# A macaron block's attention stage on one core: the two half substitutions one behind the other, a gram and four tap loads moved

## The reference

```
x = x + 0.5 * ffn(layernorm(x))
x = x + attention(layernorm(x))
x = x + 0.5 * ffn(layernorm(x))
```

```
q, k, v = silu(dwconv4(x @ Wq)), silu(dwconv4(x @ Wk)), silu(dwconv4(x @ Wv))
beta = sigmoid(x @ Wb);  q, k = l2norm(q), l2norm(k);  v, kb = v * beta, k * beta
attn = where(strict_lower, -(kb @ k.T), 0)          # one 32x32 matrix per chunk and head
T = inv(eye(32) - attn);  u = T @ v;  w = T @ kb     # unit triangular inverse
# then over the 8 chunks of a sequence, in order:
u_i = u - w @ S;  o_i = q @ S + where(lower, q @ k.T, 0) @ u_i;  S = S + k.T @ u_i
# o, v and three depthwise filters of v (3, 15, 64 taps) are five paths; their statistics
# and x go through a small gate network; the paths are mixed, normalised, projected by Wo
```

## Time and profile before

| | us |
|---|---|
| three runs, median (lowest to highest) | 455.55 (454.15 to 456.23) |
| profiled execution, its own time | 455.75 |
| its span, first to last instruction | 454.0 |

### The profile page before, as it was taken

One profiled execution on the slowest core, in us unless ns is written; L12 is line 12 of the kernel. 1 busy time (PEld: TensorE's weight loads), 2 busy tenths in 40 slices (PEclk: granted clock), 3 DMA queues, 4 the chain that ended last, 5 costly groups with the idle time before them and its releaser, 6 DMA issues.

```text
span 454.0 us, 9783 instructions
## 1 busy us (share of the span) xinstructions
PE 382.7 (84%) x4132; PEld 285.7 (63%) x4132; DVE 302.1 (67%) x461; ACT 277.5 (61%) x434; POOL 42.8 (9%) x103
## 2 busy tenths in 40 slices
PE   5599999999999799596699667936789696969996
PEld 3377776678866677495578656522256575647885
DVE  2796779547145678579849769287867696658533
ACT  4788948888597467155244306337278749457973
POOL 4000000000000100048870000000000000000000
PEclk9899999999999979679675675877689888979999
DMA  8900009200000000700060000070000000001001
GB/s 275 311 1 2 2 1 254 72 1 2 0 1 0 3 2 7 204 4 1 17 196 6 3 4 4 1 253 2 0 1 1 1 1 2 0 1 48 3 1 46
DMA packets 14325, 19.75 MB, mean 44 GB/s; under 512 B 960, under 2 KB 9152, under 8 KB 14272
## 3 DMA queue, kind: packets, MB, share of 16 engines
q1 hardware_dynamic: 14128, 18.94, 13.9%
q10 hardware_dynamic: 144, 0.01, 0.0%
HBM read 17.91 MB, written 1.05 MB: 42 GB/s over the span
## 4 chain that ended last, share of the span: by engine, by line
PE 57%; DVE 25%; ACT 10%; issue 6%; DMA 1%; DVEq 0%; SPq 0%; ACTq 0%
PE ps_a L726 11%; PE ps_a L727 11%; PE ps_a L824 6%; PE ps_a L870 3%; PE ps_d L856 2%; PE ps_a L882 2%; DVE arena L1069 2%; PE ps_a L915 2%; DVE arena L1072 2%; PE ps_d L892 2%; PE ps_d L791 2%; PE ps_a L913 2%; PE ps_a L928 2%; PE ps_d L727 2%; PE ps_d L726 2%
## 5 line engine op out<-in xcount | busy, mean ns | idle before, releaser
L726 PE MATMUL ps_a<-acts,w_f 128*128 128x512 f32 x256 | 104.2, 407 | 8.3 <-ACT acts L600 7.7
L727 PE MATMUL ps_a<-acts,w_f 128*128 128x512 f32 x256 | 102.1, 399 | 0.0
L726 PEld LDWEIGHTS ps_a<-acts,w_f 128*128 128x128 f32 x256 | 49.5, 194 | 22.0 <-ACT acts L600 9.7
L727 PEld LDWEIGHTS ps_a<-acts,w_f 128*128 128x128 f32 x256 | 49.5, 193 | 11.0 <-issue 0.7
L600 ACT ACTIVATE acts<-ps_a,vec 128x512 fp32r<-128x512 f32 x64 | 44.5, 696 | 0.0
L824 PE MATMUL ps_a<-xnp,conv_w 128*128 128x512 f32 x156 | 38.4, 404 | 0.0
L1138 DVE TENSOR_TENSOR acts<-gbuf,acts 128x512 fp32r<-128x512 f32 x32 | 21.6, 690 | 24.9 <-ACT acts L600 24.9
L1138 DVE TENSOR_TENSOR acts<-ghbuf,acts 128x512 fp32r<-128x512 f32 x32 | 21.2, 689 | 20.8 <-ACT acts L600 20.8
L824 PEld LDWEIGHTS ps_a<-xnp,conv_w 128*128 128x128 f32 x156 | 29.5, 189 | 8.5 <-issue 1.7
L985 DVE SCALAR_TENSOR_TENSOR arena<-ps_d,arena 128x512 f32<-128x512 f32 x16 | 11.0, 687 | 28.5 <-ACT arena L554 26.3
L597 ACT ACTIVATE gbuf<-ps_a,vec 128x512 f32<-128x512 f32 x32 | 22.3, 696 | 11.1 <-PE ps_a L727 11.1
(11 more groups left out here) (211 smaller groups left out, 798.5 us busy)
## 6 DMA issues: line engine op xcount, KB each, us to landing
toep<-in_fir SPq DMA_DIRECT2D x24, 288.0 KB, 5.6
w_in<-in_h SPq DMA_DIRECT2D x4, 1024.0 KB, 8.1
g_rows<-in_gW SPq DMA_DIRECT2D x4, 640.0 KB, 6.8
w_in<-in_w SPq DMA_DIRECT2D x6, 256.0 KB, 4.1
iobuf<-in_x SPq DMA_DIRECT2D x4, 256.0 KB, 6.6
toep<-in_taps SPq DMA_DIRECT2D x1, 768.0 KB, 6.5
y<-iobuf SPq DMA_DIRECT2D x3, 256.0 KB, 2.4
toep<-in_proj SPq DMA_DIRECT2D x1, 256.0 KB, 9.2
```

Source lines behind the costliest of these rows:

```text
L726: e.matmul(bank, w, hi, start=start, stop=False)
L727: return e.matmul(bank, w, lo, start=False, stop=stop)
```

## The change

Three moves, and one new wait on each of two queues. Half 0's gram (and its turn) go behind `qkv 3`, the last convolution tile; `sumsq 2` keeps its place on ScalarE and VectorE but is issued by TensorE between the first and the second quarter of `qkv 3`. VectorE does 4 steps of half 0's substitution in `solve 0` instead of 11 and 23 in `solve 2` instead of 16. GpSimd starts half 1's substitution only once `xt 0` is done (`inv_done` 1). SyncE loads tap groups 2 and 3 only once gram 1 is done. All twelve `token` steps and the eight `window` steps now stand before `fir` 4 to 7 of the order; `turn4` and the first squares stand between the `yy` steps; `xt 1` goes from before `first 0` to behind `rec 1`, and the `yy` and `aq` steps of half 1 each go one place back, so that `aq 6` follows `turn3 0`.

```diff
-SPLIT = 11
+SPLIT = 4
...
-    s += [("qkv", 2, 2), ("gram", 2, 0), ("lmat", 2, 0), ("window", 2, 4), ("window", 2, 5), ("sumsq", 2, 2),
-          ("qkv", 2, 3), ("solve", 2, 0), ("window", 2, 6), ("window", 2, 7), ("sumsq", 2, 3)]
+    s += [("qkv", 2, 2), ("window", 2, 4), ("window", 2, 5), ("sumsq", 2, 2), ("qkv", 2, 3), ("gram", 2, 0), ("lmat", 2, 0),
+          ("window", 2, 6), ("window", 2, 7), ("solve", 2, 0), ("sumsq", 2, 3)]
...
-    s += [("token", 2, i) for i in (0, 1, 4, 5, 8, 9)] + fir[4:6]
-    s += [("token", 2, i) for i in (2, 3, 6, 7, 10, 11)] + fir[6:8]
-    s += [("window", 2, i) for i in range(8, 16)]
-    for k in range(4):
-        s += [("yy", 2, k), fir[8 + k]]
-    s += [("turn4", 2, 0), ("sq", 2, 0), ("turn4", 2, 1), ("sq", 2, 1)] + sums(0) + [("sq", 2, 2)] + sums(1)
+    s += [("token", 2, i) for i in (0, 1, 4, 5, 8, 9, 2, 3, 6, 7, 10, 11)]
+    s += [("window", 2, i) for i in range(8, 16)] + fir[4:8]
+    s += [("yy", 2, 0), fir[8], ("yy", 2, 1), fir[9], ("turn4", 2, 0), ("turn4", 2, 1), ("sq", 2, 0)]
+    s += [("yy", 2, 2), fir[10], ("sq", 2, 1), ("yy", 2, 3), fir[11]] + sums(0) + [("sq", 2, 2)] + sums(1)
...
-    s += [("bo", 2, b) for b in range(4)] + [("sq", 2, 5)] + sums(4) + [("sq", 2, 6), ("xt", 2, 1)]
-    ahead = [("yy", 2, k) for k in range(4, 8)] + [("aq", 2, k) for k in range(4, 8)]
+    s += [("bo", 2, b) for b in range(4)] + [("sq", 2, 5)] + sums(4) + [("sq", 2, 6)]
+    ahead = [("xt", 2, 1)] + [("yy", 2, k) for k in range(4, 8)] + [("aq", 2, k) for k in range(4, 8)]
...
-    s += [("turn3", 2, 0), ("sq", 2, 7), ("aq", 2, 7), ("bo", 2, 4), ("bo", 2, 5), ("bo", 2, 6)]
+    s += [("turn3", 2, 0), ("sq", 2, 7), ("aq", 2, 6), ("aq", 2, 7), ("bo", 2, 4), ("bo", 2, 5), ("bo", 2, 6)]
...
             load_toep(e, 1)
+            e.wait_ge(S["pe_d"], D_AT[("gram", 2, 1)] + H)
...
             e.wait_ge(S["l_turned"], 1)
+            e.wait_ge(S["inv_done"], 1)
...
+                        if i == 3 and w == 0:
+                            sumsq(2)
-                elif kind == "sumsq":
+                elif kind == "sumsq" and i != 2:
+                    sumsq(i)
```

More of the change, by code:

```diff
@@ L767, in wo, with sumsq @@
                 e.matmul(take_d(D_AT[("wo", 2, i)]), wo_w[:, :], tile(o_c, i % 2), start=True, stop=True).then_inc(S["pe_d"], 1)
+            def sumsq(i):
+                for w in range(2):
+                    e.wait_ge(S["act_ss"], 2 * i + w + 1)
+                    e.matmul(take_d(D_AT[("sumsq", 2, i)] + w), head_w[:, :], qs[:, 6 + 2 * w + i % 2], start=True, stop=True
+                             ).then_inc(S["pe_d"], 1)
             e.wait_ge(S["consts"], 1)
```

## The result

Over the timed runs the changed kernel takes 448.34 us (median of 4, 447.03 to 449.53), the kernel before 455.25 us (median of 4); the ratio is 0.9848, 95% interval 0.9827 to 0.9869.

The account below looks back on a forecast made before the run. A chain of waits through TensorE and VectorE bounds the kernel. Early gains go nearly all back to GpSimd at `xt 1`; shorter work behind it brings `turn 0` 3.4 us earlier: profiled 455.75 becomes 452.35, forecast 452.2, range 450.2 to 456.2.

Parts of the forecast that it names:

- The waits that the prediction named: TensorE's 0.68 us before gram 0, its 4.36 in gram 1, and some 3 forecast for `xt 1` on GpSimd.
- three signs of being wrong: Gram 1's wait over 3 us, GpSimd over 38 us, or `turn3 0` more than 18 us behind `xt 1`'s end.
- Gram 0 behind `qkv 3`: Stretch ahead of gram 1: gram 1 starts at 182.7, gain 1.6 us, bounds 0 and 2.3.
- Taps behind gram 1: In gram 1: instruction wait falls to about 1.1 us, 6.9 against 10.1, gain 3.2, bounds 0 and 4.36.
- all but 0.14: Chance 0.14 went to the rival that gram 1's wait belongs to its position and stays: 3.2 us lost, 455.4.
- VectorE alone: `solve 2` up to `xt 0`: steps 8 to 30 without GpSimd take 17.8 us; `xt 0` ends at 212.9, 6.2 earlier.
- GpSimd: Half 1's substitution, started at 213.0: takes 36.8 us (bounds 36.8 and 39.3), ends at 249.9, 13.7 later than before.
- The rival that VectorE's transposes and reductions slow it: From 213 to 250: VectorE's other work slows GpSimd, ending 6.9 us later, time 459.1; chance 0.10.
- Behind `xt 1`: From `xt 1`'s end: 16.9 us to `turn3 0`, `turn 0` at 276.1 instead of 279.51; bounds 0 and 6.
- The low clock at `yy 4`: Rival: TensorE idles before `yy 4`, the clock stays low behind `xt 1`, costing 3.0 us, time 455.2; chance 0.10.

Follow-up runs that it names:

- the second profile: The changed kernel run again unchanged, against the kernel before: 449.34 us, ratio 0.9882 (0.9853 to 0.9910).

## Why the prediction was wrong

The direction was right and the size half. Two terms of the sum were too small, the gram's move (1.6 us, measured 3.4) and the taps (3.2, measured 4.5 and 3.8). The waits that the prediction named are the ones that the traces show, and none of its three signs of being wrong came, since none of them looked at the stretch ahead of gram 1.

For the first step, windows with the columns of the earlier trace rows: windows 4 and 5 and then `sumsq 2`, first in the kernel before, then in the changed one.

```profile
160.00:161.80 1.80, 1.80 (x13) 1.70 (x10) 1.22 (x2) 0.98 (x2) 0.00 (x0) 0.50 0.00 0
161.80:164.40 2.60, 2.60 (x6) 1.05 (x5) 2.07 (x3) 2.36 (x3) 0.00 (x0) 0.50 0.02 6
...
151.80:152.50 0.70, 0.70 (x8) 0.70 (x7) 0.67 (x2) 0.59 (x3) 0.00 (x0) 1.00 0.00 0
155.50:156.70 1.20, 1.20 (x4) 0.52 (x3) 0.00 (x0) 0.57 (x2) 0.00 (x0) 1.00 0.00 0
```

Step by step:

- **Gram 0 behind `qkv 3`** (1.6 us, bounds 0 and 2.3): the step that failed. It gave 3.4 us (31.21 to 27.84 and 27.81), outside its own bounds, in both profiles, and undoing it gave exactly that stretch back (31.24). I let TensorE's stretch shrink by the 0.68 us wait alone, since the low clock "now falls on `sumsq 3`". But windows 4 and 5 and `sumsq 2` now run at the full clock, ahead of `qkv 3` and inside it, and take 2.1 us together instead of 4.4. Windows 6 and 7 and `sumsq 3` got the low clock in their place, but lost only 0.9 us (from 173.99 to 177.27 before, from 168.88 to 173.10 now). Gram 0 is 0.9 us shorter (163.55 to 168.94, 5.4 us against 6.3), and the 0.68 us wait is gone. In all `sumsq 3` ended 21.2 us behind `qkv 2` (173.17 - 151.93), not 23.5. VectorE was then the one that ended last, with no idle time before 174.92: from gram 0's end to its first row of tile 3 it took 6.0 us, and my sum had 6.2. That sum was right, but it hung on a gram 0 that I let end 18.3 us behind `qkv 2`; it ended 17.0 behind it.
- **Taps behind gram 1** (3.2 us, gram 1 in 6.9): 4.5 and 3.8 (5.64 and 6.35). The term was mis-sized by adding two things that exclude each other, the 4.25 us of running at the low clock and a wait of 1.1. At the full clock it is 2.99 + 1.16 + 1.49, at the low one 4.54 + 0.16 + 1.50: one or the other hides. That it is the loads that hold TensorE back, which I gave all but 0.14, is shown from both sides (0.9901 with the wait alone, 0.9989 without it). The border of the instruction block was put near its place: 1.7 us into gram 1 by the prediction, and the packet starts 1.8 us into it (2.6 in the second profile).
- **VectorE alone** (23.3 to `xt 0`): 23.5. Right; steps 8 to 30 took 18.25 us (188.77 to 207.02) where I had 17.8.
- **GpSimd** (36.8 us, bounds 36.8 and 39.3): 246.46 - 209.10 = 37.4. Right within 0.6 us; `xt 1` waited 3.60 us, forecast about 3. The rival that VectorE's transposes and reductions slow it does not hold. Most of the 0.6 is a false mirror: I took steps 0 to 14 to cost as much as steps 16 to 30, but with none of VectorE's substitution beside them they take 18.15 us (209.10 to 227.25) and the others 17.68. So of the 18.81 us that steps 0 to 14 took beside VectorE only 0.7 were lost to it, not 1.2. The rule that the prediction cites from the Trainium skill ("SBUF — State Buffer", Who interferes with whom) agrees: between 209 and 246 us VectorE has no instruction with two inputs in SBUF and GpSimd is not slowed, while each multiply and subtract of its substitution has two. (The section leaves VectorE's two-port modes out of what it says on one input, which the prediction does not say.)
- **Behind `xt 1`** (16.9, then 7.25): 16.4 and 16.7, then 7.4 and 7.7. Near. The low clock at `yy 4` came (0.50 from 248.50 to 250.30), but did not lengthen the stretch. No run took the three instruction blocks away by themselves, so that they make up this gain is argued, not shown.

The rest of the distance to 448.34 I take for luck of one set (the second gave 5.1 us of gain, where the six stretches say 4.9 to 6.0). My range was too narrow below for a sum whose two largest terms were both taken at the low side.

What stays open: the taps wait alone is worth 4.5 us and the whole change 5.1 to 6.9, so the gram's move, the split, GpSimd's wait and the order bring 0.6 to 2.4 together, and the intervals do not tell more. Without the gram move they seem to cost something: 0.9952 against 0.9901 for the taps alone, in one set, with intervals that just overlap. The profiles say the same and show where it goes. The kernel before with the tap wait alone has 121.4 us in the six stretches, the changed kernel 120.4 and 121.5. Up to `xt 0`'s end the changed kernel is 4.0 to 4.7 us ahead of it, and from there to `turn 0` it falls back by 3.7 to 4.1, since it waits for GpSimd.

## What to carry to other kernels

When TensorE stands in a run of small matmuls and the trace calls it "issue", look at the DMA share beside it and at the packets of the instruction queue before anything else: moving a bulk load behind that run was worth more here than all the reordering of work. Parts of a schedule can be worth nothing or less one by one and pay only together (the gram's move needed the small split, the small split needed GpSimd late, GpSimd late needed `xt 1` behind `rec 1`), so price each under the others; the last of these links rests on the rows of two kernels, not on a run with that order alone undone. And re-read who ends last after each step: the wait moved from GpSimd to ScalarE's queue within two edits.

## What the runs showed of the hardware

Eight loads of 288 KB beside a run of 32x32 matmuls held TensorE for 3.84 to 5.79 us in one go, until 1 us before the end of the loads (187.69) or about 2 us behind it; four loads, through before the matmuls ran dry, added nothing (2.07 against 2.08). What waits is the packet on the instruction queue: it starts 1.8 to 2.6 us into gram 1 in the eleven profiles without these eight loads in its way and 4.1 to 6.1 us into it in the three with them, and in the twelve profiles in which gram 1 stands, TensorE goes on 2.3 to 2.6 us behind the packet's start. The kernels without these loads had gram 1 in 5.6 to 6.5 us at either level of the clock (5.78 at 0.54, 6.35 with its first 210 matmuls at 0.98), so about 22 to 26 ns a matmul. Since the clock makes no difference, I take it that the arrival of instructions sets this, which no run varied by itself. Some kernels also spread more from run to run, and I can't say why: with the loads beside gram 1 450.0 to 455.3 over 12 runs, but with SPLIT 11 and the loads behind it 450.5 to 455.9 too, against 448.6 to 450.2 over 6 for the changed kernel.
